# Attention's softmax sum on VectorE: fold six partial sums to three, then sum three, in place of one sum of six

## The reference, cut to what matters

```
h = conv_relu_batchnorm(x)                          # 16 x 746 x 128
h = h + delta_rule_attention(layernorm(h))
h = h + expert_choice_ffn(layernorm(h))             # 16 experts
h = h + video_attention(layernorm(h), video_embeds) # this case
h = h + top2_ffn(h)                                 # 8 experts
```

```
logits  = einsum('avhd,bthd->abhvt', k, q) / sqrt(64)   # v: 12 frames of the video
weights = softmax(logits, axis=3)                        # over the 12 frames
attn    = einsum('avhd,abhvt->abhtd', v, weights)        # then the mean over the videos
```

## Time and profile before

| | us |
|---|---|
| median of three executions | 2290.06 |
| the profiled execution | 2295.13 |
| its span, first to last instruction | 2293.3 |
| DVE busy in the whole span | 1628.0 (71%) |
| PE busy in the whole span | 2010.1 (88%) |
| ACT, POOL busy in the whole span | 1072.4 (47%), 605.2 (26%) |
| attention stage, first maximum to last output copy | 1073.1 to 1542.6 |

### The profile page before, as it was taken

One profiled execution on the slowest core, in us unless ns is written; L12 is line 12 of the kernel. 1 busy time (PEld: TensorE's weight loads), 2 busy tenths in 40 slices (PEclk: granted clock), 3 DMA queues, 4 the chain that ended last, 5 costly groups with the idle time before them and its releaser, 6 DMA issues. The chain is left out here.

```text
span 2293.3 us, 54560 instructions
## 1 busy us (share of the span) xinstructions
PE 2010.1 (88%) x20890; PEld 1782.7 (78%) x20890; DVE 1628.0 (71%) x4095; ACT 1072.4 (47%) x2698; POOL 605.2 (26%) x650
## 2 busy tenths in 40 slices
PE   6699999989636988886999999976999999999998
PEld 5588777778535877884777777765999999999998
DVE  4755556554583755665999999987777777777773
ACT  4433333332344555543666666642444444444443
POOL 0002222220025555511333333333212221221220
PEclk9699999999878999997999999996999999999999
DMA  8100001100211111100000000000000000000000
GB/s 184 42 1 12 11 11 14 14 6 1 76 55 40 42 35 39 39 14 1 3 3 3 3 3 3 3 3 1 8 7 14 7 7 14 7 7 14 7 8 14
DMA packets 80354, 44.50 MB, mean 19 GB/s; under 512 B 45800, under 2 KB 74024, under 8 KB 79752
## 3 DMA queue, kind: packets, MB, share of 16 engines
q1 hardware_dynamic: 74248, 29.53, 5.7%
q0 software_dynamic: 5888, 12.07, 2.0%
HBM read 27.20 MB, written 14.38 MB: 18 GB/s over the span
## 5 line engine op out<-in xcount | busy, mean ns | idle before, releaser
L2127 ACT ACTIVATE w<-banks,b 128x384 f32<-128x384 f32 (+1 forms) x512 | 259.4, 571 | 393.6 <-PE banks L2201 393.6
L2183 PE MATMUL banks<-w,w 128*128 128x128 f32 (+1 forms) x3072 | 364.1, 275 | 0.0
L2183 PEld LDWEIGHTS banks<-w,w 128*128 128x128 f32 (+1 forms) x3072 | 350.4, 189 | 9.1 <-issue 8.7
L1710 PE MATMUL banks<-qT,w 64*64 64x128 f32 (+1 forms) x4608 | 268.1, 269 | 21.7 <-DVE eb L1612 18.5
L1710 PEld LDWEIGHTS banks<-qT,w 64*64 64x64 f32 x4608 | 247.4, 134 | 39.6 <-issue 20.6
L1718 PE MATMUL banks<-eb,w 64*64 64x128 f32 (+1 forms) x4608 | 269.0, 270 | 1.8 <-DVE eb L1612 1.7
L1681 POOL TENSOR_TENSOR t<-eb 128x768 f32<-128x768 f32 x96 | 170.2, 1773 | 309.2 <-ACT eb L1658 306.0
L1718 PEld LDWEIGHTS banks<-eb,w 64*64 64x64 f32 x4608 | 244.0, 133 | 2.5 <-DVE eb L1612 2.5
L2024 DVE SCALAR_TENSOR_TENSOR h<-banks,t_wt,h 128x128 f32 (+3 forms) x672 | 183.7, 343 | 83.2 <-PE banks L2183 79.7
L1237 POOL DMA_INDIRECT xg<-xs,rowu x184 | 181.5, 987 | 128.6 <-DMA xg<-xs,rowu 86.6
L2199 PE MATMUL banks<-t_xh,t_w1h 128*128 128x384 f32 (+1 forms) x512 | 182.5, 357 | 0.0
(11 more groups left out here) (305 smaller groups left out, 4268.4 us busy)
## 6 DMA issues: line engine op xcount, KB each, us to landing
out<-h SPq DMA_DIRECT2D x16, 320.0 KB
xs<-r_xl SPq DMA_DIRECT2D x16, 192.0 KB, 2.9
h<-in_xT SPq DMA_DIRECT2D x4, 750.0 KB, 15.2
h<-in_xT SPq DMA_DIRECT2D x4, 749.0 KB, 18.2
xg<-xs,rowu POOLq DMA_INDIRECT x184
xs<-r_xl SPq DMA_DIRECT2D x16, 128.0 KB
blocks<-NT SPq DMA_DIRECT2D x24, 48.0 KB, 1.9
D<-blocks SPq DMA_DIRECT2D x24, 48.0 KB, 2.0
```

Source lines behind the costliest of these rows:

```text
L1710: last = nc.tensor.matmul(lbanks(n)[place(n, hd), v, 0:wide(n)], k.Kt[half(hd), v, :], qT[half(hd), n // NC % 2, (n % NC) * P:(n % NC) * P ...
L2127: nc.scalar.activation(gb[u % 2][:, f, s * GW:s * GW + NFREE[s]], k.ps[:, order.bank(n), 0:NFREE[s]], ACT.Relu, bias=k.b1_1[:, 2 * e + f:2 ...
L2183: last = nc.tensor.matmul(k.psf[0:n, o:o + P], gb[u % 2][:, f, c * P:c * P + n], k.w2_1[:, 2 * e + f, :], start=(f == 0), stop=(f == 1))
```

## The change

The sum of six becomes two instructions. DVE first adds frames 3 to 5 of `t1` to frames 0 to 2 into a new tile `t2` (3 x 128 numbers), waits for its own semaphore `folded`, and sums three. POOL's wait for a free `t1` buffer is for `folded` and no longer for `summed`.

```
+        t2 = sb("t2", [P, 3, P])
-        logged = sem("logged")
+        logged, folded = sem("logged"), sem("folded")
...
                         dve.wait_ge(tree, w + 1)
                         m = wide(w)
+                        nc.vector.tensor_tensor(t2[:, :, 0:m], t1[:, w % 2, 0:3, 0:m], t1[:, w % 2, 3:6, 0:m],
+                                                ALU.add).then_inc(folded, 1)
+                        dve.wait_ge(folded, w + 1)
                         if w >= 2:
                             dve.wait_ge(logged, w - 1)
-                        nc.vector.tensor_reduce(den[:, w % 2, 0:m], t1[:, w % 2, :, 0:m].rearrange("p v t -> p t v"),
-                                                AX_X, ALU.add).then_inc(summed, 1)
+                        nc.vector.tensor_reduce(den[:, w % 2, 0:m], t2[:, :, 0:m].rearrange("p v t -> p t v"), AX_X,
+                                                ALU.add).then_inc(summed, 1)
...
                     if n >= 2:
-                        pool.wait_ge(summed, n - 1)
+                        pool.wait_ge(folded, n - 1)
```

## The result

The changed kernel takes 2277.78 us (median of six, 2273.08 to 2280.96) against 2290.92 us for the kernel before in as many runs: a ratio of 0.9942, 95% interval 0.9928 to 0.9956. The direction was right, the size was not.

What follows compares the result with a forecast made beforehand. Attention alternates between DVE's own pace and holds by other engines; two sums a period, 0.18 us, give 2.7 over 15 periods, plus 0.5 and 0.1: 3.3 us, from 2290.06 to 2286.8. Range for 8 in 10: 2279 to 2301.

Steps and rivals of the forecast that it cites:

- What bounds the kernel: Attention stage: DVE never idle, but GpSimd holds some multiplies, so only two of six sums per period lie on the path.
- Rival A: Attention stage: every sum's saving counts, 7.7 us, 2282.4; or, with a cheaper sum of three, 2278; the latter given 0.15.
- The fold and its wait: DVE, each full chunk: adding 384 pairs from SBUF costs 551 ns, the wait for its own semaphore 34 ns.
- The sum of three: DVE, each full chunk: 153 ns fixed plus 384 numbers at 1.042 + 0.72 ns, 830 ns in all.
- The lower bound: Sum of three on DVE: no surcharge for spread numbers, 553 ns, or -0.37 us per full chunk.
- the second half of rival A: Sum of three at its lower bound, two sums per period: -0.74 us a period, 11.8 us, 2278; chance 0.15.
- B: Sum of three: surcharge goes by result, 1107 ns, 2301 us; or the 1507 floor stays, 2330; chance 0.11.
- C: Sixth chunk: GpSimd's add gets ahead of the fold and delays it, 1.5 us in each of 15 periods, 2312; chance 0.07.
- the add of the sixth chunk: GpSimd's add, starting 0.29 us after the fold, held about 0.25 us: recorded with about 1.8 instead of 1.55 us.
- The earlier release: GpSimd's wait for a free `t1` on `folded`: worth nothing, since its adds wait for ACT's exponentials, not DVE.

Runs made afterwards that it cites:

- e2: The changed kernel plus one unused VectorE sum of 256 numbers between fold and sum of three: 2287.5 us, ratio 0.9989 to the kernel before.
- e4: The kernel before, no fold, with GpSimd writing each token's six numbers side by side for one sum of six: 2275.3 us, ratio 0.9931.
- e1: The changed kernel plus 72 VectorE sums and additions of various layouts behind the attention stage; whole time not compared, three frames 512 bytes apart took 593 ns.
- e5: The changed kernel plus other VectorE instructions and 12 GpSimd additions behind the attention stage; whole time not compared, a multiply begun during an addition took 2.87 us.
- e7: The changed kernel, fold kept, with GpSimd's addition split in two parts: 2273.4 us, ratio 0.9926 to the kernel before.
- e3: The changed kernel with GpSimd waiting for `summed` again instead of `folded`: 2278.5 us, ratio 0.9944 to the kernel before.

## Why the prediction was wrong

**What bounds the kernel** held. DVE busy 440.00 of 440.00 hid holds by GpSimd, and two of six sums lay on the path. e2, e4 and the changed kernel itself give three sizes of the same: periods shorter by 0.31, 1.11 and 0.71 for savings per sum of 0.13, 0.57 and 0.34. Rival A's first reading, that every sum counts, falls by each of them.

**The fold and its wait** were priced right: 551 and 34 ns against 546 and 40 (1228.94 plus 0.54 to 1229.52).

**The sum of three** is the step that failed: 830 ns against 595. The prediction took 0.72 ns from the old sum and from L297 and laid it on each of the 384 numbers. Both rows pay for every read, L297 with its numbers 24 bytes apart (e1 has 328 ns for that step too), the old sum with its six frames. Three frames, with the tokens 4 bytes apart, do not. That both gave 0.72 to the last digit was chance in part: with the other engines quiet six frames pay 0.64. With 595 in place of 830 the working of the prediction gives 0.33 us per sum, and 0.34 was measured; 15 periods of 0.68 and six last sums of 0.34 are 12.2 us, the stage's measured 12.2 (10.0 up to the last maximum before the last sequence, 2.2 behind it).

**The range** knew it, but gave it too little. The lower bound, no surcharge (553), was written down with its consequence of 2278, as the second half of rival A, with 0.15 for the rival; and the range ended at 2279, a microsecond short of that figure. The agreement of two rows was taken to hold for every spread read; neither had three streams.

**B and C** did not come. B's surcharge per result falls by e1, where three frames cost 593 ns and not 1107. No fold was recorded above 0.56 us, and GpSimd was not held by it: the add of the sixth chunk is recorded with 1.55 us and not the 1.8 foretold, 0.63 after the fold's start instead of 0.29 after the sum's. DVE had moved earlier against PE and ACT, by the 0.34 us of the sum before; the prediction had kept the fold where the sum had been. A smaller step was wrong there too: it charged the add with the whole overlap. In e2 they overlap by 0.12, and the add takes 1.56; a hold costs the overlap less 0.14 (e5, e7). e7 shows that the hold is real where the overlap is longer. No run has the fold start behind an addition, so what C priced stays unmeasured.

**The earlier release** of the buffer is worth nothing (e3), as said.

## What to carry to other kernels

When a price is carried over from one shape to another, ask on which side of a step each shape may lie. Two rows that agree bound only what they share; a term for which no row has the new shape deserves the chance of its bound, and if the bound decides the size of the result, the range should be drawn around it. Before folding a slow sum over spread numbers, try to have the producer write them side by side: here that alone was worth more than the fold (18.5 us of the stage against 12.2). And an engine that is never idle may yet be standing in another's way: compare one instruction's durations along a period, and what ends when it is long.

## What the runs showed of the hardware that was not expected

- A sum on DVE over frames 512 bytes apart in SBUF, with the tokens side by side, is nearly free of surcharge for two and three frames (4 and 40 ns on 128 results) and pays 0.63 to 0.65 ns for every number from four frames on (1019, 1445, 2725 ns for 4, 6, 12; e1). With the tokens 16 bytes apart two and three frames pay as well (632 and 845 ns; e5).
- In the running kernel the old sum of six took 1507 ns; the same shape with the other engines quiet took 1445, and 1516 with the frames 528 bytes apart, where 576 gave 1444. Neither difference is explained.
- GpSimd writing its results 24 bytes apart costs 19 ns in 1818 (e4).
- A GpSimd addition that starts just behind a DVE multiply with two SBUF inputs is recorded with 3.24 us instead of 1.80 (e5): the wait stands in its duration, not ahead of it. The one that is held gets back 0.14 us of the overlap, on either engine (e5, e7), so that an overlap of 0.12 costs nothing (e2).
